# A two-layer graph attention network: edge count and first projection merged into one block, layers written out

## What is computed

```python
x = layernorm(x) * ln_g + ln_b                      # the LayerNorm that feeds the layers
for l in range(2):
    q = ((x @ Wq[l].T + bq[l]) * scaling).reshape(n, H, DH)
    k = (x @ Wk[l].T).reshape(n, H, DH)
    v = (x @ Wv[l].T).reshape(n, H, DH)
    scores = einsum('ehd,ehd->eh', q[tgt], k[srcidx])       # one score per edge and head
    w = softmax of scores over the edges of one target
    agg = segment_sum(w[:, :, None] * v[srcidx], tgt)
    x = batchnorm(x + agg.reshape(n, D) @ Wo[l].T + bo[l])
    x = batchnorm(x + relu(x @ W1[l].T + b1[l]) @ W2[l].T + b2[l])
x = layernorm(x)                                    # then the small network on x
```

## Time and profile before

| | us |
|---|---|
| time, median of 3 runs | 1222.61 (1222.03 to 1223.6) |
| time of the profiled execution | 1221.42 |
| its span | 1219.5 |
| PE busy | 1069.1 (88%) |
| DVE / ACT / POOL busy | 784.3 / 573.5 / 437.7 |
| set-up and edge count | 0 to 203 |
| projection, layer 0 | 217 to 311 |
| attention, layer 0 | 313 to 608 |
| output block, layer 0 | 608 to 692 |
| projection, layer 1 | 692 to 784 |
| attention, layer 1 | 786 to 1081 |
| output block, layer 1 | 1081 to 1162 |
| final block | 1162 to 1219.5 |

### The profile page before, as it was taken

One profiled execution on the slowest core, in us unless ns is written; L12 is line 12 of the kernel. 1 busy time (PEld: TensorE's weight loads), 2 busy tenths in 40 slices (PEclk: granted clock), 3 DMA queues, 4 the chain that ended last, 5 costly groups with the idle time before them and its releaser, 6 DMA issues. The chain is left out here.

```text
span 1219.5 us, 20276 instructions
## 1 busy us (share of the span) xinstructions
PE 1069.1 (88%) x6736; PEld 882.7 (72%) x6737; DVE 784.3 (64%) x2449; ACT 573.5 (47%) x1054; POOL 437.7 (36%) x482
## 2 busy tenths in 40 slices
PE   3778686799899999999999699999999999989833
PEld 2545454798778888888698699777888888879721
DVE  6565564232667777777477624376777777748878
ACT  5423322210456666666533311176666666633335
POOL 5654575000334444444212200044444444302314
PEclk9887988899999999999999899999999999999956
DMA  6010114754561222213210453482131211330153
GB/s 133 21 41 21 41 42 140 186 120 96 125 156 35 58 50 50 41 35 119 70 35 6 151 114 88 102 195 63 35 70 37 55 35 35 102 104 1 64 119 87
DMA packets 53392, 93.79 MB, mean 77 GB/s; under 512 B 15794, under 2 KB 34094, under 8 KB 53048
## 3 DMA queue, kind: packets, MB, share of 16 engines
q1 hardware_dynamic: 53268, 92.63, 30.6%
q10 hardware_dynamic: 36, 0.01, 0.0%
HBM read 37.55 MB, written 24.17 MB: 51 GB/s over the span
## 5 line engine op out<-in xcount | busy, mean ns | idle before, releaser
L790 POOL TENSOR_SCALAR probs<-probs,mass_inv 125x1250 f32<-125x1250 f32 x160 | 211.2, 1320 | 337.3 <-DVE mass_inv L914 337.3
L809 PE MATMUL banks<-k_stack,q_stack 128*125 128x416 f32 (+1 forms) x960 | 295.6, 393 | 5.9 <-DMA q_stack<-q_split 4.7
L905 DVE CUSTOM_DVE_ANT_0 probs<-banks,scores_bias 125x416 f32<-125x416 f32 (+1 forms) x480 | 267.1, 582 | 14.9 <-PE banks L809 10.6
L823 PE MATMUL banks<-ident,probs 125*125 125x125 f32 x1600 | 259.5, 277 | 8.0 <-DVE probs_t L896 5.8
L823 PEld LDWEIGHTS banks<-ident,probs 125*125 125x125 f32 x1600 | 241.5, 188 | 31.7 <-issue 21.9
L875 ACT ACTIVATE probs<-probs,neg_peak 125x1250 f32<-125x1250 f32 x160 | 213.4, 1334 | 57.7 <-DVE neg_peak L928 57.7
L864 ACT ACTIVATE probs_t<-banks 125x500 f32<-125x500 f32 x320 | 152.6, 477 | 113.3 <-PE banks L823 113.2
L838 PE MATMUL banks<-probs_t,v_pair 125*64 125x250 f32 x1600 | 186.2, 379 | 0.9 <-ACT probs_t L864 0.9
L809 PEld LDWEIGHTS banks<-k_stack,q_stack 128*125 128x125 f32 x960 | 144.5, 189 | 34.5 <-issue 14.7
L475 PE MATMUL banks<-onehot_src,onehot_dst 125*125 125x512 bf16 x540 | 120.3, 386 | 33.0 <-POOL onehot_dst L290 20.4
L838 PEld LDWEIGHTS banks<-probs_t,v_pair 125*64 125x64 f32 x1600 | 107.5, 136 | 54.3 <-ACT probs_t L864 1.3
(11 more groups left out here) (248 smaller groups left out, 1464.6 us busy)
## 6 DMA issues: line engine op xcount, KB each, us to landing
q_stack<-q_split SPq DMA_DIRECT2D x160, 125.0 KB, 2.3
scores_bias<-edge_bias SPq DMA_DIRECT2D x8, 1171.9 KB
edge_bias<-bias SPq DMA_DIRECT2D x10, 585.9 KB
k_stack<-k_hi SPq DMA_DIRECT2D x16, 312.5 KB, 4.0
k_stack<-k_lo SPq DMA_DIRECT2D x16, 312.5 KB, 5.4
resid<-residual SPq DMA_DIRECT2D x2, 2500.0 KB, 10.1
residual<-t SPq DMA_DIRECT2D x8, 625.0 KB, 2.9
values<-v_stage SPq DMA_DIRECT2D x2, 2400.0 KB
```

The lines of the kernel that those rows point to most:

```text
L790: nc.gpsimd.tensor_scalar(probs[:, u % 4, :], probs[:, u % 4, :], mass_inv[:, u % 4:u % 4 + 1], 1.0, ALU.mult, ALU.mult).then_inc(att["pro ...
L809: mm = nc.tensor.matmul(pb[0:NT, t % 5, 0:sn], q_stack[:, n % 2, half, part, tile * NT:(tile + 1) * NT], k_stack[:, head * N + s0:head * N ...
L823: mm = nc.tensor.transpose(pb[0:NT, 5 + t % 2, j * NT:(j + 1) * NT], probs[:, u % 4, (j0 + j) * NT:(j0 + j + 1) * NT], ident[0:NT, 0:NT])
L905: nc.vector.tensor_tensor_reduce(out=probs[:, slot % 4, s0:s0 + sn], in0=pb[0:NT, t % 5, 0:sn], in1=scores_bias[:, (n % GROUPS) * GROUP + ...
```

## The change

**One block for the count and layer 0's projection.** The counts get one set of three banks, and the projection of layer 0 the other five (`BANKS`); the order of its jobs is values first, then queries, then keys. PE alternates: `counting(j)` for tile j, then the work that the gap behind it holds. Behind tiles 0 and 1 stand all five turns of the normed input (`GAP_TURNS`); behind tile 1 also the turns of Wv, behind tiles 2 to 8 what `GAP_ENDS` gives (three values; two values and the turns of Wq; three values; two values and a query tile; four, three and three query tiles), and behind tile 9 the rest, with all the keys. `counting(j)` first waits for `bias_ready` of the tile before, since there is only one set of count banks. The loops over tiles are written out in Python on PE, ACT and DVE; only the loops over rounds stay. `own`, targets and one-hots are made as before, but DVE does round 0 of the next tile ahead of the loop, then `combine`, then the low parts of the gap's jobs.

**Evacuation.** Queries are evacuated by ACT with a scaled bias (`bq_scaled`), values by ACT twice (`v_pair`, `v_stage`); DVE makes only low parts. The key buffers `k_hi` and `k_lo` are doubled, with two semaphores `k_stored`.

**Shift.** All ten tiles of the shift of x are POOL's, between its targets of tiles 0 and 1 and those of tiles 2 to 9.

**Layers written out.** The loop over layers is a Python loop. Layer 1's projection block has the job order of before. In the last layer `h_hi`, `h_lo` and the residual are not made or stored, and Wk is not loaded again; the loads of w_in, w_out, constants and `x_in2`, and the splitting of w_in, stand in the last output block instead of the final block, and the product with `w_out` stands ahead of the turn of tile 6.

```diff
+        JOBS = (turns("wv") + V_JOBS[0:5] + turns("wq") + V_JOBS[5:] + Q_JOBS[:-1] + turns("wk") + Q_JOBS[-1:] + K_JOBS,
+                turns("wk") + K_JOBS[0:6] + turns("wq") + K_JOBS[6:] + Q_JOBS[0:6] + turns("wv") + Q_JOBS[6:] + V_JOBS)
+        BANKS = (range(3, 8), range(0, 8))
+        GAP_TURNS = {0: (0, 1), 1: (2, 3, 4)}
+        GAP_ENDS = (0, 4, 7, 13, 16, 19, 23, 26, 29, len(JOBS[0]))
...
-                with pe.Fori(0, TILES // 2) as jj:
-                    spans = spans_of(pe, 2 * jj, 2)
...
+                def counting(j):
+                    [(first, rounds, before)] = spans_of(pe, j)
+                    if j:
+                        pe.wait_ge(bias_ready, j)
...
+                for j in range(TILES):
+                    counting(j)
+                    for jj in GAP_TURNS.get(j, ()):
+                        turned(jj)
+                    for t in gap_jobs(j):
+                        if t == 0:
+                            pe.wait_ge(h_split, 2 + TILES)
+                        project(pe, 0, t)
...
+            @block.vector
+                for j in range(TILES):
+                    [(first, rounds, before)] = spans_of(dve, j)
+                    for k in range(RING):
+                        step(j, first, before, 0, k)
...
+                    if j:
+                        combine(j - 1)
+                        for t in gap_jobs(j - 1):
+                            if JOBS[0][t][0] in SPLIT:
+                                reduced(dve, 0, t)
+                    if j == 3:
+                        scaled_bias(dve)
+                    with dve.Fori(1, rounds) as q:
+                        for k in range(RING):
+                            step(j, first, before, q, k)
...
+            @block.scalar
+                for j in range(TILES):
+                    logs(j)
+                    for jj in GAP_TURNS.get(j, ()):
+                        kept(jj)
+                        if jj + 1 < TILES // 2:
+                            normed(jj + 1)
+                        lower(jj)
+                    for t in gap_jobs(j):
+                        projected(act, 0, t)
...
+            @block.gpsimd
+                targets(0, 2)
+                pool.wait_ge(shift_in, 16)
+                pool.wait_ge(h_ready, TILES)
+                for k in (1, 0):
+                    shift(nc.gpsimd, PARTS_X[k]).then_inc(x_shifted, 1)
+                targets(2, TILES)
...
+            @block.sync
+                bias_out(0)
+                residual(0, 4)
+                residual(4, TILES)
+                bias_out(1)
+                sp.wait_ge(proj["filled"], DC)
+                sp.dma_start(w_nat[0]["wk"][:, :, :], weight(gnn["Wk"], DC)[:, 0:DC, :]).then_inc(wk_in, 16)
+                shifted(1)
+                shifted(0)
+                for j in range(2, TILES):
+                    bias_out(j)
+                sp.wait_ge(proj["copied"], len(V_JOBS) + len(Q_JOBS))
+                for k in range(2):
+                    sp.wait_ge(bias_stored[k], 32 * (TILES // 2))
+                first_bias(sp)
+                for n in range(2):
+                    stacked(sp, n)
+                for c in range(DC):
+                    k_stacked(sp, 0, c)
+                sp.wait_ge(k_stored[0], 64 * (DC // 2))
...
-        with nc.Fori(0, LAYERS) as layer:
+        for layer in range(LAYERS):
...
+                    @block.vector
+                    def _(dve):
+                        scaled_bias(dve)
+                        for t, job in enumerate(JOBS[layer]):
+                            if job[0] in SPLIT:
+                                reduced(dve, layer, t)
...
+        def scaled_bias(dve):
+            dve.wait_ge(proj["vec"], 128)
+            nc.vector.tensor_scalar(bq_scaled[:, :], vec[:, BQ:BQ + DC], float(DH) ** -0.5, None, ALU.mult).then_inc(proj["bias_q"], 1)
...
-                    high(1, DC - 2, h_hi, t2)
+                    if not last_layer:
+                        high(1, DC - 2, h_hi, t2)
```

More of the change, by code:

```diff
@@ L147, in gnn_ffn @@
[L147 to L155, removed]
@@ L168, in gnn_ffn @@
+        log_bias = place2("log_bias", [NT, 1], F32, 4)
+        assert r2[0] <= sizes["R2"]
+        counts = pb[0:NT, 0:3, :].rearrange("p a b -> p (a b)")
         wk_in = sem("wk_in")
@@ new lines, in gnn_ffn, with clear, weight, products @@
+        oph = {k: sem("o_" + k) for k in ("wo", "w1", "w2", "res", "filled", "hi", "done", "a_hi", "a_lo", "asked", "root",
+                                          "t_done", "h1_hi", "h1_lo", "h1_lo_last", "r_hi", "r_lo0", "r_lo1", "h_hi", "h_lo", "h_lo_last", "g_done", "step")}
+        def clear(engine, sems):
+            for s in sems:
+                engine.sem_clear(s)
+        def weight(w, c):
+            return w.rearrange("l (c p) i -> p (l c) i", p=P)
+        def products(kind, chunks):
+            return [(kind, c, n) for c in chunks for n in range(3)]
@@ new lines, in k_stacked @@
+        def k_stacked(sp, layer, c):
+            sp.wait_ge(proj["done"], split_count(layer, JOBS[layer].index(("k", c, 2)) + 1))
+            for half in range(2):
+                own, other = slice(half * DH, half * DH + DH), slice((1 - half) * DH, (1 - half) * DH + DH)
+                cols = slice((2 * c + half) * N, (2 * c + half + 1) * N)
+                sp.dma_start(f32(k_stack[own, cols]), f32(k_hi[c % 2][own, :])).then_inc(k_stored[c % 2], 16)
+                sp.dma_start(f32(k_stack[other, cols]), f32(k_lo[c % 2][own, :])).then_inc(k_stored[c % 2], 16)
@@ new lines, in logs @@
+                def logs(j):
+                    act.wait_ge(counts_ready, j + 1)
+                    act.wait_ge(log_ready, j)
+                    nc.scalar.activation(more[:, :], counts[:, 0:N], ACT.Relu).then_inc(more_ready, 1)
+                    act.wait_ge(more_ready, j + 1)
+                    if j >= 2:
+                        act.wait_ge(bias_stored[j % 2], 32 * (j // 2))
+                    nc.scalar.activation(bias_row[:, j % 2, :], more[:, :], ACT.Ln, bias=log_bias[:, :]).then_inc(log_ready, 1)
@@ L438, in _ @@
+                combine(TILES - 1)
+                for t in gap_jobs(TILES - 1):
+                    if JOBS[0][t][0] in SPLIT:
+                        reduced(dve, 0, t)
             @block.tensor
@@ L1229, in part @@
-        def part(k):
-            return slice(SPANS[k][0], SPANS[k][-1] + 1)
-        def sets(k):
-            return slice(2 * SPANS[k][0] // SET, 2 * (SPANS[k][-1] + 1) // SET)
+                    if not last_layer:
+                        low(dve, nc.vector, DC - 1, t2, h_hi, h_lo, "h_hi", "h_lo_last")
         with nc.Block(no_gpsimd_drain=True) as block:
```

936 lines of the change are left out of this document (469 added, 467 removed).

## The result

| | before | after |
|---|---|---|
| time, median of 4 runs, us | 1223.11 (1222.03 to 1224.27) | 1205.97 (1205.05 to 1207.14) |
| ratio | | 0.9856, 95% interval 0.9835 to 0.9878 |
| profiled execution / span, us | 1221.42 / 1219.5 | 1207.14 / 1205.4 |

A forecast was written before the change was run, and what follows sets the result against it. PE was taken to bound layer 0's projection but not the count, where some 43 us of PE idle left room. 1221.4 + 14.5 (layer 0) + 8.8 (layer 1's start) - 11.5 (end) = 1233.2, predicted 1233, range 1214 to 1249.

The forecast's parts named there:

- the cost x of a count: Layer 0's merged block, tiles 3 to 9: head, bank-setting matmuls and 54 matmuls, 16.4 us each, bounds 14.5 to 17.4.
- the first rival: Seven tiles run well: short head, round 1's one-hots keep pace, x = 14, sum 1216; chance 0.22.
- its sign of being wrong: Prediction wrong if x is off by more than 1.5, or key stores do not stand on the path.
- The head, 2.7: PE's idle at each count's loop head in layer 0, taken as 10.8 / 4 = 2.7 us.
- At best 54 x 0.23 = 12.4: Claimed best time of the 54 matmuls in one tile's count: 12.4 us.
- The 13.0: Time taken for a count's 54 matmuls, with round 1 waiting for DVE and POOL: 13.0 us.
- the 8 us forecast: Ahead of tile 2's count: a new PE wait of about 8 us for POOL, beyond PE's own work.
- E + 49: Layer 0's attention start, E being the last count's end; SP's order and key stores hold it: 327.7 against 313.2.
- Layer 1's start: Layer 1's projection: DVE's work stands behind all eight vectors, +8.8 us, from 7 to 10.
- The end: Last output block and final block: -11.5 us, from -13 to -8.
- -6.2 and -5.1: The end: -6.2 from L1132 (-3.5) and DVE's last h_lo with barrier (-2.7); -5.1 in the final block.
- The third: Rival: DVE's one-hot bursts starve POOL every tile, x = 17.4 and attention at E + 52, 1243; chance 0.2.

The follow-up runs named there:

- e5: The kernel before with the loop over tile pairs written out on PE alone: 1221.44 us, ratio 0.9984.
- e6: The kernel of e4 with DVE loading the table entry of one tile at a time, not two per pair: 1207.55 us, ratio 0.9854.
- e3: The changed kernel with nothing in the gaps behind tiles 2 to 8, all values and queries behind tile 9: 1243.67 us, ratio 1.0155.
- e1: The changed kernel with SP storing the first two key chunks between the first and second query group: 1203.41 us, ratio 0.9829.
- e8: The changed kernel with SP storing both query groups and key chunks 0 to 2 ahead of the bias reads: 1200.63 us, ratio 0.9806.
- e2: The changed kernel with layer 1's vector wait and scaled bias on DVE moved behind the first three key tiles: 1194.59 us, ratio 0.9763.
- e4: The kernel before with the loops over tile pairs written out on PE, ACT and DVE: 1212.86 us, ratio 0.9907.
- e10: The unmerged kernel of e6 with POOL_STEPS = 1, so POOL makes fewer small one-hots: 1200.84 us, ratio 0.9828.
- e7: The changed kernel with POOL_STEPS = 1: POOL makes small one-hots of steps 0 to 2 only, DVE the rest: 1192.86 us, ratio 0.9755.
- e9: The changed kernel with the edits of e7 and e2, and SP's bias reads between the two query groups: 1177.66 us, ratio 0.9633.

## Why the prediction was wrong

**The failed step is the cost x of a count** in tiles 3 to 9, "x = 16.4", with bounds 14.5 to 17.4. It measured 12.8: 12.6 from the first matmul to the last, and a mean head of 0.2. That is below even the first rival's 14, and off by more than the 1.5 that the prediction itself gave as its sign of being wrong. Seven of them cost 89.8 us and not 114.8, so 25.0 of the 28.4 us by which the start of layer 0's attention was missed are this step. The other 3.4 are small terms of the same front, and the later stretches were 2.7 longer than forecast; that the two nearly cancel is luck. Three parts of x were off:
- *The head, 2.7.* It was 0 in six of the seven tiles and 1.34 ahead of tile 4. I took the mean idle of four loop heads as the price of a head, whatever stands ahead of it. Where PE has queued products to run, the head costs no PE time (tile 3 above); behind transposes or work that itself had to wait it costs 0.8 to 1.6 (tiles 1, 2 and 4). Part of the fall is the loop written out: in the kernel before that alone takes the four heads from 10.8 to 7.1 us (e5). That the head's register work runs beside queued matmuls is my reading of these rows; no run takes it apart on PE. On DVE, e6 does: halving the table work halved the longest head.
- *"At best 54 x 0.23 = 12.4."* This was no floor. The 0.23 came from a stretch granted 0.81 of the clock on average; the second row of the same group, 18 in 3.38, already gave 0.19, so 10.1 for 54. In e3, where an idle stands at the head again, round 0 is back at 6.68.
- *POOL's waits.* The 13.0 left 0.6 for them above that floor. They are 1.7 us a tile (0.90 + 0.78 in tile 3), as tile 8 had shown (1.61). Matmuls and waits together are 11.9, so here two errors of opposite sign left 1.1 too much.

The trace of the kernel before already held a tile of 12.8 us from first matmul to last, tile 2, which ends at 67.8 and of which the sum made no use:

```profile
54.97 0.71 PE L466 MATMUL banks<-minus_one,one_row 1*125 1x512 bf16 x3 [1.73 <-issue]
...
64.25 3.38 PE L475 MATMUL banks<-onehot_src,onehot_dst 125*125 125x512 bf16 x18 [0.36 <-POOL onehot_dst L290]
```

**Two steps of layer 0 held.** Tile 2 was forecast to start at 94.0 and did at 92.65, behind POOL's shift (11.2 us, 11.4 forecast). Tile 1's 15.9, which the prediction names but does not work out, came close too: its count ends at 64.7, against 63.7. Of the 8 us forecast between PE's own work and it there were 4.5 (88.2 to 92.65): the head 0.83, the matmuls that set the banks 1.29, and 2.35 as a wait for POOL. The attention was forecast at E + 49 and came at E + 47.5, with PE waiting on keys. e1 and e8 show that it was SP's order, and that it is the bytes ahead that count: issued soon behind the bias reads a chunk takes 16.8 us to free its buffer (e1), issued ahead of them 8.3 (e8).

**Layer 1's start held**: +8.8 forecast, +8.2 measured, and 7.8 of it is there by the first key's evacuation (18.5 us behind DVE's last h_lo, 10.7 before). e2 gives 11.9 back by moving one wait. That is more than the 8.2, because PE's 3.9 us sooner start lay hidden behind the wait, as I had said, and comes out once it is moved.

**The end came out near, in part by luck**: -11.5 forecast, -12.3 measured (the forecast's own terms, -6.2 and -5.1, make -11.3). Up to PE's first turn of the final block 5.8 us went, against the 6.2, but not as I had them. Three late L1132 went and not two; I had left out the longest:

```profile
1144.60 2.51 DVE L1132 SCALAR_TENSOR_TENSOR tiny<-mv,tiny,vec 128x1 f32<-128x1 f32 x1
```

They give 5.8 where I had 3.5. The 2.7 for DVE's last h_lo and the barrier did not come: from the end of DVE's last step on t to PE's first turn it was 2.5 us before and is 2.4 now. In the final block 6.6 us went, with the waits on x_in and w_out gone. No run undid this part; it is read off the traces.

**Not forecast:** the two attention stages, +4 us together. Of this 3.0 are PE being busy longer for the same work (288.1 against 286.6 us in layer 0, 286.7 against 285.1 in layer 1), at a lower granted clock: the first 26.8 us of layer 0's attention had 0.91 against 1.00, and layer 1's has a stretch of 3 us at 0.50 (823 to 826) that before's profiled execution does not have. But e4 and e5, which have the attention code of before, show 294.6 and 294.8 for layer 1's stage too, where that execution had 292.9, and e10 takes 294.9 at 1.00 with PE busy 285.4. So this change need not be the cause, and the clock is not all of it. This stays open.

**The first rival was the right mechanism**, priced too high. It had chance 0.22. The third, that POOL starves every tile, fell: the triples took 2.2 to 3.0 us beside DVE's one-hots, not 6. The kernel before could have told: of its triples in the count two took 6.0 us (at 39.38 and 188.10), and the others 1.75 to 3.2. In tile 8:

```profile
172.34 2.53 POOL L290 TENSOR_SCALAR onehot_dst<-own,target_col 125x125 bf16<-125x125 f16 x3 [0.20 <-POOL target_col L287]
```

The rule that the prediction takes from the Trainium skill ("SBUF — State Buffer", Who interferes with whom) speaks of one instruction that holds the shared pair. That every triple waits out a whole burst of one-hots was my step from it. Two triples of the kernel before did, with DVE busy for all of their 6.0 us; the others did not.

**What the merging is worth.** The forecast asked what the merged block gives and did not ask what writing the loops out gives alone. e4 and e6 answer: the kernel that keeps the two blocks apart reaches the attention at 299.2 and 298.1, the merged one at 299.3. So what the merged kernel gains in layer 0, the written-out loops reach alone; on top of them the merging gave nothing. With POOL relieved in both, the merged one is 4.1 us ahead in one profiled execution each (e7, e10), and e9 reaches 283.5 with an order on SP that e10 does not have. The merged block also differs in its evacuation, its single set of count banks and the place of POOL's shift; no run takes these apart.

## What to carry to other kernels

Before a mean idle or a mean duration goes into a sum, look at what stood ahead of it: a loop head behind queued work and a matmul at full granted clock are other numbers than those of an engine that had run dry, and a lower bound must come from the fastest row, not from a typical one. When a change both restructures and writes loops out, price the writing out alone first. And read the order of one DMA queue by bytes: a key chunk issued soon behind the large bias reads here took twice as long to land as one ahead of them. Last, a wait for a small late load does not belong ahead of work that doesn't need it.

## What the runs showed that was not expected

- The longest idle ahead of DVE's pairs was not the loop's branch: with the loop written out it stayed at 7.1 us (7.4 before), and loading one table entry instead of two brought it to 3.2 (e4, e6).
- Writing the pair loop out on PE alone gave 0.9984; on PE, ACT and DVE together 0.9907 (e5, e4).
- POOL's triples beside DVE's one-hots took 2.2 to 3.0 us in the merged kernel, against 1.75 alone, and the 6.00 of the earlier trace rows has only one like it in the whole count before; with one of the two triples taken from POOL the attention starts 14 us earlier (e7).
- Stretches with the same code were 1 to 4 us longer in e4, e5 and e6 than in the profiled execution of the kernel before (layer 1's attention 294.3 to 294.8 against 292.9), in part by PE at a lower granted clock.
